# A transformer block with a GRU on one Trainium2 core: the attention's first queries in whole banks, and the expert layer with its shared expert first, row-major sums and weights by way of DRAM

## What is computed

```python
h = gru_scan(cond_2048, x, W_ih, W_hh, b_ih, b_hh)     # 256 steps, state (4, 256)
q, k, v = heads(h @ Wq + bq), heads(h @ Wk + bk), heads(h @ Wv + bv)   # 16 heads of 128
x = x + (softmax(q @ k.T * scale + causal) @ v) @ Wo + bo
y = adaln_attention(x, cond_2048, ...)                 # second attention, 16 heads of 16
probs = softmax(y @ gate_w.T)                          # 16 experts
topk_w, topk_idx = top_k(probs, 4); topk_w /= topk_w.sum()
combine = one_hot-weighted sum of topk_w               # (1024 tokens, 16 experts)
shared = (silu(y @ Sg) * (y @ Su)) @ Sd * sigmoid(y @ shared_gate_vec.T)   # 704 hidden
for e in range(16):                                    # 176 hidden each
    sparse += (silu(y @ Eg[e]) * (y @ Eu[e])) @ Ed[e] * combine[:, e]
x = x + shared + sparse
```

## Time and profile before

| what | value |
|---|---|
| median of 3 runs | 1084.39 us |
| profiled execution, its own time | 1083.47 us |
| its span, first to last instruction | 1081.3 us |
| GRU, up to the attention's first instruction | 457.4 us |
| expert layer, from L1555 to the end | 822.0 to 1081.3 us |
| busy share of the span: PE, DVE, ACT, POOL | 88%, 62%, 51%, 50% |
| mean granted TensorE clock | 0.773 |
| DMA over the span | 28 GB/s |

### The profile page before, as it was taken

How to read it: one execution, slowest core, us unless ns; L and a number is a source line. 1 busy time by engine, 2 the same in 40 slices (tenths; PEclk the granted TensorE clock), 3 DMA queues, 4 the chain that set the end, 5 groups by cost and what they waited for, 6 DMA issues and landing times. The chain is left out here.

```text
span 1081.3 us, 33994 instructions
## 1 busy us (share of the span) xinstructions
PE 951.9 (88%) x13386; PEld 674.3 (62%) x13386; DVE 666.0 (62%) x2544; ACT 546.5 (51%) x1792; POOL 539.6 (50%) x1245
## 2 busy tenths in 40 slices
PE   3989999999999998679999999576985999999997
PEld 3777777777777777548888887444444444444443
DVE  5866666666666666677777777746855445454554
ACT  4544444444444444447777777566762333333432
POOL 1266666666666666615555553285002555555551
PEclk8555555555555555579999999988997999999999
DMA  6100000000000000020000100100000111112111
GB/s 267 42 4 4 3 4 3 4 3 3 4 4 3 4 3 4 2 81 31 31 31 31 31 2 2 35 3 2 1 1 18 35 60 58 51 51 68 51 51 39
DMA packets 9017, 30.28 MB, mean 28 GB/s; under 512 B 1446, under 2 KB 3112, under 8 KB 8492
## 3 DMA queue, kind: packets, MB, share of 16 engines
q1 hardware_dynamic: 8876, 28.32, 7.8%
HBM read 27.27 MB, written 1.05 MB: 26 GB/s over the span
## 5 line engine op out<-in xcount | busy, mean ns | idle before, releaser
L423 POOL COPY gp<-hq 128x16 f16<-128x16 f16 x256 | 69.1, 270 | 174.5 <-DVE hq L413 174.5
L306 ACT ACTIVATE r_scan<-gr 128x8 f32<-128x8 f32 x256 | 46.6, 182 | 180.3 <-PE gr L218 180.3
L432 POOL TENSOR_TENSOR q_part<-q_raw,q_part 128x64 f16<-128x64 f32 x238 | 111.6, 469 | 19.2
L398 DVE TENSOR_REDUCE z_sum<-gz 128x8 f32<-128x16 f32 x256 | 44.8, 175 | 120.6 <-PE gz L218 120.0
L218 PEld LDWEIGHTS gr<-hq,w_two 128*128 128x128 f16 x1024 | 47.4, 107 | 115.0 <-DVE hq L408 109.9
L218 PE MATMUL gr<-hq,w_one 128*128 128x4 f16 x2048 | 117.6, 166 | 0.0
L273 PE MATMUL gq<-gp,wq_part 128*128 128x64 f16 x1428 | 114.4, 237 | 0.0
L218 PE MATMUL gr<-hq,w_two 128*128 128x4 f16 x1024 | 68.7, 171 | 51.6 <-DVE hq L408 28.8
L924 POOL TENSOR_SCALAR probs<-probs,rinv 128x128 f32<-128x128 f32 (+1 forms) x128 | 53.0, 427 | 119.5 <-DVE rinv L820 119.5
L430 POOL CAST q_part<-q_raw 128x64 f16<-128x64 f32 x238 | 108.6, 456 | 0.0
L218 PEld LDWEIGHTS gr<-hq,w_one 128*128 128x128 f16 x2048 | 94.1, 103 | 0.0
(11 more groups left out here) (257 smaller groups left out, 2687.8 us busy)
## 6 DMA issues: line engine op xcount, KB each, us to landing
wf_ffn<-in_wf SPq DMA_DIRECT2D x28, 448.0 KB, 3.3
raw_attn<-in_pairs SPq DMA_DIRECT2D x8, 770.0 KB, 4.4
shared<-in_wq SPq DMA_DIRECT2D x1, 2056.0 KB, 12.3
xT<-in_xT SPq DMA_DIRECT2D x1, 1024.0 KB, 7.7
x<-in_xr SPq DMA_DIRECT2D x1, 1024.0 KB, 6.6
out<-fin SPq DMA_DIRECT2D x4, 256.0 KB, 2.5
whh<-in_whh SPq DMA_DIRECT2D x1, 768.0 KB, 4.7
wih<-in_wih SPq DMA_DIRECT2D x1, 768.0 KB, 6.8
```

The lines of the kernel that those rows point to most:

```text
L306: nc.scalar.activation(r_scan[:, 2::3], R[bp][:, k * 8:(k + 1) * 8], ACT.Sigmoid, scale=1.0 / GS).then_inc(t_in, 1)
L398: nc.vector.tensor_reduce(z_sum[:], Z[bp][:, k * 16:(k + 1) * 16] .rearrange("p (m q) -> p m q", q=2), AX.X, ALU.add).then_inc(z_sum_ready, 1)
L423: nc.gpsimd.tensor_copy(gp[:, :, :, :, t].rearrange("p q j b -> p q (j b)"), hq[:, nxt, :, 2::3]).then_inc(h_stored, 1)
L432: nc.gpsimd.tensor_tensor(q_part[:, 1, h, :, :, c], src, q_part[:, 0, h, :, :, c], ALU.subtract).then_inc(q_split, 1)
```

## The change

In the attention's prologue the 18 left queries are made in one go, in three sets (8, 8 and 2) that fill a bank each; ScalarE reads all 18 into a larger `q_raw`; VectorE splits a set with one copy and one subtraction. The first scores no longer wait for them (the wait moves to the first unit that needs them, 52 units on). Two of the three sets are split after the first units' keys, values and scores. The first values use the banks `acc[3]` and `acc[2]`. `big` is one buffer in place of three, and `squares` lies on `q_raw`.

In the expert layer the hidden rows begin with the shared expert's. Its gate is a product with a vector broadcast to 128 columns (`gv`), so it comes out the same on all partitions (`gate`). The experts' weights are transposed after unit 3 (`cwT`), stored to DRAM (`cw_rows`), and loaded back with one row broadcast to all partitions of its expert (`cw_of`, three buffers); `hT` multiplies with these in place of the bank `CB`. `summed` has the hidden values as the stationary operand and sums tokens by features, so there is no transposing after the loop. The loops are written out rather than looped on the engines.

```diff
-            left_queries(range(4))
+            for n, (h, columns) in enumerate(left_sets):
+                for at, c in enumerate(columns):
+                    out = acc[n][:, at * B * QB:(at + 1) * B * QB].rearrange(...)
...
+                mm.then_inc(q_psum, 1)
             pe.wait_ge(first_split["k"], 1)
-            for n in range(2):
-                keys(n, first_keys[n])
+            keys(0, first_keys[0])
             pe.wait_ge(first_split["v"], 1)
...
-            pe.wait_ge(q_split, left)
-            pe.wait_ge(v_ready, 2)
+            values(0, first_values[0])
+            keys(1, first_keys[1])
+            values(1, first_values[1])
+            pe.wait_ge(k_ready, 1)
             scores(0)
+            pe.wait_ge(q_read, left)
+            values(2, first_values[2])
+            pe.wait_ge(k_ready, 2)
+            values(3, first_values[3])
             pe.wait_ge(bo_ready, 1)
+            pe.wait_ge(v_ready, 3)
...
+            left_queries(0)
+            key_lo(0, first_keys[0])
+            value_lo(0, first_values[0])
+            key_lo(1, first_keys[1])
             maxima(0)
+            value_lo(1, first_values[1])
             inverse(0)
+            value_lo(2, first_values[2])
+            value_lo(3, first_values[3])
+            left_queries(1)
+            left_queries(2)
...
+                if n == first_mixed:
+                    sp.wait_ge(cwT_ready, 2)
+                    sp.dma_start(cw_rows, cwT[:]).then_inc(cw_stored, 16)
+                    sp.wait_ge(cw_stored, 16)
+                    sp.wait_ge(gate_ready, 2)
+                if n - NB >= first_mixed:
+                    sp.wait_ge(h_made, 2 * (n - NB) + 2)
+                for a, b, who in pieces(n):
+                    src = gate[a:b, :] if who == E else cw_rows[who:who + 1, :].to_broadcast([b - a, NT])
+                    sp.dma_start(cw_of[a:b, n % NB, :], src).then_inc(cw_in[n % NB], 16)
...
+            def summed(u):
+                c, hf = u // 2, u % 2
+                for k in range(4):
+                    i = 4 * hf + k
+                    for n, (h, w) in enumerate(((h_hi, w_hi), (h_hi, w_lo), (h_lo, w_hi))):
+                        mm = pe.matmul(acc[i // 2][:, i % 2 * D:(i % 2 + 1) * D],
+                                       h[:, u % 2, k * P:(k + 1) * P], w[:, c % 2, 4 * P:6 * P],
...
+            for hf in range(2):
+                for j in range(J):
+                    mm = pe.matmul((MB, UB)[hf][:], gv[:, j, :], yT[:, j, halves[hf]],
+                                   start=(j == 0), stop=(j == J - 1))
+                mm.then_inc(gate_psum, 1)
...
-                    pe.matmul(CB[:], select[:, par, :], cwT[:, halves[hf]],
-                              start=True, stop=True).then_inc(c_psum, 1)
+                if u == CW_AT:
+                    pe.wait_ge(cw_ready, 1)
+                    for i in range(TILES):
+                        mm = pe.transpose((LB, MB)[i // 4][0:E, (i % 4) * P:(i % 4 + 1) * P],
+                                          cw[:, i, :], ident[:])
...
-                    nc.vector.tensor_tensor(hT[:, k % 2, :], CB[:], prod[:, k % 2, :],
-                                            ALU.mult).then_inc(h_made, 1)
+                weight = gate[:, halves[hf]] if c < first_mixed else cw_of[:, c % NB, halves[hf]]
+                nc.vector.tensor_tensor(hT[:, u % 2, :], prod[:, u % 2, :], weight,
+                                        ALU.mult).then_inc(h_made, 1)
...
+                    if c >= 2:
+                        pool.wait_ge(free, 2 * (c - 2) + 2)
```

More of the change, by code:

```diff
@@ L481, in attention_block @@
         w_part = {n: sb(f"w{n}_part", [P, 2, 2, W], FP16) for n in PARTS}
-        big = {n: sb(f"w{n}_big", [P, W]) for n in PARTS}
+        big = sb("w_big_a", [P, W])
         k_bias = sb("k_bias", [P, 2, 2])
@@ L1495, in ffn_block @@
         y_lo = sb("y_lo", [P, J, NT], FP16)
-        lg = sb("lg", [P, TILES, R17])
+        gate = sb("gate", [P, NT])
+        cw_of = sb("cw_of", [P, NB, NT])
+        lg = sb("lg", [P, TILES, E])
         mx = sb("mxr", [P, TILES])
@@ L1528, in ffn_block @@
[L1528 to L1532, removed]
+        lg_psum, chain, exps, cw_ready = (sem(n) for n in ("lg_psum", "chain", "exps", "cw_ready"))
+        gate_psum, gate_ready = sem("gate_psum"), sem("gate_ready")
+        cwT_psum, cwT_ready, cw_stored = sem("cwT_psum"), sem("cwT_ready"), sem("cw_stored")
@@ L1534, in ffn_block, with owner, pieces, shared_only @@
         halves = [slice(0, HALF), slice(HALF, NT)]
+        def owner(row):
+            return E if row < SHARED else min((row - SHARED) // INTER, E - 1)
+        def pieces(c):
+            rows = [owner(c * P + p) for p in range(P)]
+            cuts = [p for p in range(P) if p == 0 or rows[p] != rows[p - 1]] + [P]
+            return [(a, b, rows[a]) for a, b in zip(cuts, cuts[1:])]
+        def shared_only(c):
+            return all(who == E for _, _, who in pieces(c))
+        first_mixed = min(c for c in range(NCH) if not shared_only(c))
@@ L1536, in _ @@
+        cw_count, loads = {}, [0] * NB
+        for c in range(first_mixed, NCH):
+            loads[c % NB] += 16 * len(pieces(c))
+            cw_count[c] = loads[c % NB]
         @block.sync
         def _(sp):
[L1538 to L1542, removed]
+            for c in range(NCH):
+                if c + 2 < NCH:
+                    sp.wait_ge(d_ready, c + 1)
+                    sp.dma_start(wf[:, c % 2], dram["wf"][c + 2]).then_inc(wf_in[c % 2], 16)
+                n = c + 2
+                if first_mixed <= n < NCH:
+                    if n == first_mixed:
[8 more added lines that the diff above has]
+                        sp.dma_start(cw_of[a:b, n % NB, :], src).then_inc(cw_in[n % NB], 16)
@@ L1551, in _, with product @@
         def _(pe):
-            pe.wait_ge(w_in, 32)
+            def product(dst, c, first, hf, ready):
+                n = 0
+                for j in range(J):
+                    cols = slice((first + j) * P, (first + j + 1) * P)
+                    for w, y in ((w_hi, y_hi), (w_hi, y_lo), (w_lo, y_hi)):
+                        mm = pe.matmul(dst[:], w[:, c % 2, cols], y[:, j, halves[hf]],
+                                       start=(n == 0), stop=(n == 3 * J - 1))
+                        n += 1
+                mm.then_inc(ready, 1)
@@ L1560, in _ @@
[L1560 to L1567, removed]
-                mm = pe.matmul(acc[a][:], w_hi[:, 1, 4 * P:5 * P], h_hi[:, 1, :], start=True,
-                               stop=False, skip_group_check=True)
@@ L1570, in _ @@
-            mm.then_inc(d_done, 1)
-            pe.wait_ge(ct_done, 2)
-            pe.wait_ge(y_lo_ready, 2)
-            def product(dst, par, c0, hf, ready):
-                n = 0
-                for j in range(J):
-                    cols = slice((c0 + j) * P, (c0 + j + 1) * P)
-                    for w, y in ((w_hi, y_hi), (w_hi, y_lo), (w_lo, y_hi)):
-                        mm = pe.matmul(dst[:], w[:, par, cols], y[:, j, halves[hf]],
-                                       start=(n == 0), stop=(n == 3 * J - 1))
-                        n += 1
-                return mm.then_inc(ready, 1)
@@ new lines, in _ @@
+            for u in range(units):
+                c, hf = u // 2, u % 2
+                if hf == 0:
+                    pe.wait_ge(gu_ready, c + 1)
+                if u < 2:
+                    pe.wait_ge(y_lo_ready, hf + 1)
+                if u:
+                    pe.wait_ge(g_act, u)
+                product(GB, c, 0, hf, g_psum)
+                if u:
+                    pe.wait_ge(prod_ready, u)
+                else:
+                    pe.wait_ge(gate_ready, 2)
+                product(UB, c, J, hf, u_psum)
+                if u == CW_AT:
[3 more added lines that the diff above has]
+                                          cw[:, i, :], ident[:])
+                    mm.then_inc(cwT_psum, 1)
+                if u:
+                    if hf:
+                        pe.wait_ge(d_ready, c + 1)
+                    pe.wait_ge(lo_ready, u)
+                    summed(u - 1)
@@ L1622, in _ @@
+            pe.wait_ge(lo_ready, units)
+            summed(units - 1)
         @block.scalar
@@ L1721, in _ @@
[L1721 to L1730 removed]
+            dve.wait_ge(lg_psum, 1)
@@ L1732, in _ @@
+            for a in range(4):
+                dve.wait_ge(d_done, units - 1 + a // 2)
+                nc.vector.scalar_tensor_tensor(out=fin[:, 2 * a:2 * a + 2, :].rearrange("p i d -> p (i d)"),
+                                               in0=acc[a][:], scalar=1.0 / (HS * WS),
+                                               in1=x1[:, 2 * a:2 * a + 2, :].rearrange("p i d -> p (i d)"),
+                                               op0=ALU.mult, op1=ALU.add).then_inc(fin_ready, 1)
         @block.gpsimd
@@ new lines, in _ @@
+            for c in range(NCH):
+                par = c % 2
+                pool.wait_ge(wf_in[par], 16 * (c // 2 + 1))
```

(15 more changed lines are left out.)

366 lines of the change are left out of this document (132 added, 234 removed).

## The result

| | before | change |
|---|---|---|
| median, us | 1084.26 (4 runs) | 1053.38 (4 runs, 1052.11 to 1055.99) |
| ratio, 95% interval | | 0.9716 (0.970 to 0.9732) |
| profiled span, us | 1081.3 | 1050.9 |

Faster by 30.9 us; forecast were 1052.5 us and 31.9. The four times of the change lie within 3.9 us, the four of before within 1.6. That is too few to say that the change scatters more: 15 later times of the kernel before, beside `e1_prologue_only`, lie within 4.1 us.

The account below looks back on a forecast made before the run. TensorE was taken to bound the expert loop, VectorE waits and the slow clock the prologue. Gains 8.0 + 9.7 + 11.2 + 3.0 = 31.9 us from 1083.47 give 1051.6; plus 0.9 for the median, 1052.5 us, range 1046 to 1063.

Parts of the forecast that it names:

- TensorE holds the loop, one for one: Expert loop: work taken off TensorE is gained in full, 11.2 us, between 2.5 and 12.
- The sum of 12 smaller matmuls costs the same: Expert loop: 12 matmuls of 256 columns take the same 1.31 us as 6 of 512.
- rival B: Prologue gains 4 rather than 8 us and the sums lose 4 to 8.6: 1060 to 1065 us; chance 0.11.
- No stall behind `hT`: Expert loop: beside GpSimd's split, 0.5 of the 0.8 us margin before h_lo is needed is used; stall 0.
- rival A: Expert loop: hT waits for GpSimd's whole split every second unit, 25 us, 1077.7 us; chance 0.14, whole or half.
- Start of the experts: From the logits to unit 2 of the expert loop: gain 9.7 us, between 6 and 12.
- Prologue: Attention's prologue: reordered matmuls bring unit 1's transposes to some 480 from 488.08, gain 8.0 us, between 4 and 9.
- a fall in the gap near 477: Attention's prologue: the clock falls in that gap, a case for the low end of the gain, 4 us.
- rival D: TensorE stays at the low clock through prologue and gate, losing 4 and 3 us: 1059.5 us; within the forecast's 0.70.
- Clock 1.00 from about 464 on: Sign expected in the profile: TensorE at the full clock from about 464 us, in the attention's prologue.
- rival C: Expert loop: broadcast rows land too late if a load takes 24 us or more, 1085 to 1110 us; chance 0.04.
- The end: After the last sum: reading out and transposing go, two additions of 0.65 us follow directly; gain 3.0 us.

Follow-up runs that it names:

- e1_prologue_only: The kernel before with only the change's attention block: 1076.13 us, ratio 0.9932.
- e3_spread_back: The change with one float16 matmul of 512 columns put back in each unit from unit 6 on, 50 in all: 1063.24 us.
- e9_change_again: The change itself run again, unaltered, on one chip with two later kernels: 1052.55 us.
- e2: The change with the attention block of the kernel before: 1059.51 us, ratio 0.9791.
- e4: The change with hT's operation done twice on VectorE in every unit: 1083.56 us.
- e5: The change with hT done twice, and GpSimd leaving out w_big and w_lo from chunk 2 on: 1055.41 us.
- e7: The change with the last ten of the 18 left query columns split by GpSimd in the loop, every second unit from unit 8: 1050.70 us.
- e6_columns_inner: The change with the head column as inner index in the three wide query splits: 1049.86 us.
- e6_again: The change with the head column innermost in the wide query splits, run again on one chip with the change: 1050.48 us.
- e8_inner_and_late: The change with the head column innermost, and the two late query sets split after the second unit's maxima: 1051.22 us.

## Why the prediction was right, point by point

- **TensorE holds the loop, one for one:** right, 11.2 us forecast and measured, shown by `e3_spread_back` (9.9 us for an expected 10.8).
- **The sum of 12 smaller matmuls costs the same:** right, 1.31 us, so rival B's second half did not come.
- **No stall behind `hT`:** right, but with less room than argued. I had 0.3 us for `hT`'s wait and 0.2 for `h_lo`'s, 0.5 of 0.8; measured are 0.45 and 0.18, and 0.2 are left. The rule from the Trainium skill (SBUF — State Buffer, "Who interferes with whom"), that the second waits for the first to end, describes the rows of the loop: `hT` behind one operation in the change, behind `w_lo` whole when it is made twice. It does not describe the row from which rival A came: that operation ended at 828.42, `w_lo` at 827.53, and GpSimd began two more operations in between (827.51 and 827.88). In the profile of `e1_prologue_only` the same operation took 1.36 us in the same way. Why it lost to GpSimd's next operations stays open. A wait of `hT` for all of `w_lo`, which is rival A's mechanism, does occur, but only with `hT` made twice, where it cost 30 us together with the added work; the 25 us of rival A itself were not tested.
- **Start of the experts, 9.7:** measured 8.3. The mis-sized term is the logits and the gate together, 9.05 us forecast and 10.57 measured. In this profile the gate took 5.17 us (5.0 forecast) and the logits, which I called unchanged, 4.05 before and 5.40 after, because the clock fell some 2 us into them; in the kernel before it was still full at 822 to 824, and fell at about 825, near their end. First the windows of the kernel before, then the change's:

```profile
822.00:824.00 2.00, 2.00 (x18) 2.00 (x19) 1.01 (x4) 1.98 (x2) 1.94 (x4) 1.00 0.00 0
824.00:826.00 2.00, 2.00 (x16) 1.92 (x15) 0.00 (x0) 0.00 (x0) 2.00 (x6) 0.81 0.00 0
...
814.50:816.50 2.00, 2.00 (x18) 2.00 (x18) 0.99 (x1) 1.92 (x2) 1.92 (x3) 0.92 0.00 0
817.00:819.00 2.00, 2.00 (x11) 2.00 (x11) 1.83 (x1) 0.00 (x0) 2.00 (x2) 0.50 0.00 0
824.00:826.00 2.00, 2.00 (x9) 0.84 (x8) 1.86 (x17) 0.94 (x2) 0.18 (x1) 1.00 0.39 124
```

TensorE is busy throughout (2.00 of 2 us), so the fall comes some 2 us into unbroken work; before 814.44 it had waited at times, at the full clock (1.39 us busy from 812 to 814). How the time falls on the two is not fixed. The change's second profile, `e9_change_again`, has it the other way round:

```profile
815.98 4.38 PE fb L1598 x32
820.37 6.23 PE fb L1603 x8
```

Nor is the sum a property of the change: logits and gate together took 10.6 us in seven of the profiles here (the change's and those of `e2`, `e3`, `e4`, `e5`, `e7` and `e9`), 8.9 in those of `e6_columns_inner` and `e6_again`, 12.2 in that of `e8_inner_and_late`.
- **Prologue, 8.0:** measured 7.1, and two of its steps failed and cancelled, which is luck. The clock was at 1.00 through 461.20 to 472.00, so the queries took 1.6 us less. And the two late sets cost VectorE 4.2 us (472.37 to 476.59), not 2.2. So the second maxima ended at 477.4, just where the forecast had them, by another way. The 0.9 us that is missing lies behind them: the second keys took 2.74 us at the low clock where the forecast had 1.3, a case that its range had named (a fall in the gap near 477). The luck is that of one profile, too. In `e9_change_again`, the same kernel, the clock rose later and the queries took 5.92 us rather than 4.94. The prologue took 24.39 us to unit 1's transposes, against 23.39 in the first profile and 30.63 in the kernel before: a gain of 6.2 us rather than 7.2.

  The price of the splits has its own reason. I priced an operation of 512 elements by `h_lo`'s 0.71, a row with another access pattern. The nearer rows were the single query columns of the kernel before, which have this pattern:

```profile
468.20 0.29 DVE L827 CAST q_part<-q_raw_a 128x64 f16<-128x64 f32 x1
468.53 0.43 DVE L829 TENSOR_TENSOR q_part<-q_raw_a,q_part 128x64 f16<-128x64 f32 x1
```

64 elements took 0.29 us to copy and 0.43 us to subtract, so eight of them at once were not bound to cost little more than one. What followed is what the kernel before suffered from, on a smaller scale: a wait on VectorE and slow keys behind it.
- **The clock (rival D):** it came in part. The clock was low over the second keys and over part of the logits and the gate, at 1.4 and 1.5 us over the forecast; it was not low through the whole prologue, as rival D had it. "Clock 1.00 from about 464 on" failed as a sign for the same reason, and unit 2 of the expert loop stands at 832.07 rather than 830.
- **The broadcast rows through DRAM are hidden (rival C):** right. Before the run the nearest row was a plain load; now

```profile
cw_of<-cw_rows SPq DMA_DIRECT2D x9, 512.0 KB, 3.7
```

3.7 us against the 24 from which it would have decided.
- **The end, 3.0:** 3.3 measured. The 4.5 us in its working do not follow from the two times beside them (1073.7 to 1077.64 is 3.9); they do with the 0.60 us that the chain of the kernel before shows on VectorE's queue behind the last addition.
- **The whole:** the sum was 1.5 us too high against the two spans (31.9 and 30.4). The largest term, the loop, was right by its mechanism, and so was the end; that prologue and start were off by only 0.9 and 1.4 us is in part luck.

## To carry to other kernels

A loop that one engine bounds gives back one for one what that engine sheds, until the next chain's slack is used up. Work out that slack with contention, since here 0.7 us more on VectorE in each unit cost 30 us, the whole gain. Price a strided operation by a row with the same pattern, not by one with the same number of elements: turning the order of elements of the copy and the subtraction halved both.

## What was not expected of the hardware

- 512 elements of float16 written at a step of 32 bytes took 1.25 us (copy) and 2.30 us (subtraction, which also reads one operand at this step); in runs of 8 neighbours 0.58 and 1.04.
- In the profile of `e3_spread_back` the granted clock is recorded as 1.00 through the GRU, 0.50 in all others, and the GRU was no shorter: the attention began at 457.85 us there, at 457.57 in the change, and between 456.65 and 458.34 in all the profiles. Seven runs without a trace also have a mean clock of 0.97 to 0.98 on record, the others about 0.77, and none of the seven is the fastest of its kernel. If the record is true, the recurrent stage does not care for TensorE's clock. That was not tried apart.
- The same stretch (logits and gate) varied by 3.3 us between kernels that differ only 330 us earlier. How much of the scatter from run to run this is stays open.
